# A fused attention and feed-forward kernel: first-batch stack copies moved in SP's queue, weight preparation moved to POOL, the batch loop written out

## The chip, the cores and the metric

One core of a Trainium2 chip. The metric is the time of one launch in microseconds (us), as the device reports it; lower is better. Engines: TensorE (PE in the profile, PEld its weight loads), VectorE (DVE), ScalarE (ACT), GpSimd (POOL), and SyncE (SP), which here only issues DMAs.

## What is computed

16 batches of 256 tokens with 512 features go through an attention block whose input is scaled and shifted by a condition vector, and then through a feed-forward block with ternary weights:

```
scale, shift = split(emb @ W_emb + b_emb)
xn = rms_norm(x) * g_norm * (1 + scale) + shift
q, k, v = heads(xn @ W_qkv)                  # 16 heads of 32
q, k = rms_norm(q) * g_q, rms_norm(k) * g_k
attn = softmax(q @ k.T * 32 ** -0.5)
o = attn @ v
y = o + o @ W_out
h = gelu(quant(layer_norm(y)) @ ternary(w_fc).T)
out = x + quant(layer_norm(h)) @ ternary(w_proj).T
ternary(w) = sign(round(w / mean(|w|))) * mean(|w|)
```

Everything is float32 at the boundary. Products are kept exact enough by splitting an operand into a float16 part "hi" and a float16 rest "lo".

## The kernel before

Each engine has its own instruction stream, written out by hand; semaphores order them. One iteration i works on several batches at once: the last products of batch i-2 (`late`), the feed-forward block of i-1 (`ffn`), the attention of i (`att`), Q, K and V of i+1 (`qkv`), and the rms norm of i+2 (`pre`). Iterations run from -2 to 17. `run` (line 434) calls them; iterations 3 to 13 are one body in a loop (`Fori`) on every engine, the others are written out.

An iteration has a first half (y = o + o @ W_out, norms, row maxima of the logits in four groups, eight units of the feed-forward block) and a head loop over h = 0 to 15: scores of head h on TensorE (line 831), exp and p_hi on ScalarE (1118, 1124), p_lo on VectorE (1448), products with v on TensorE (846 to 848). Scores of head h wait for the p_lo of two heads before, since they share a PSUM bank. Into the head loop the tables at lines 56 to 102 put other work by head number: pieces of Q, K and V (`FILLER`, and `SECOND_FILLER` for iteration 0), square sums, norms, transposes through the bank `T`, and in iteration 0 the preparation of the ternary weights: rounding (1037 on ScalarE, 1223 on VectorE), cutting (1232, 1234), signs (1048).

The first batch has no earlier batch to hide behind. Iteration -1 computes its Q, K and V while the weights are still coming in; iteration 0 takes the row maxima and then its scores. Scores are products of a stack `stk`: q and k parts of all heads, copied there by 16 DMAs from `qkT` (lines 570, 572), and one row with the negated maxima, `mrow` (written by VectorE at line 1420), copied by one DMA (`maxima_row`, 518). SP issues all DMAs in program order. Ahead of the stack copies of iteration -1 stand two for the rms norm of batch 1: the row `rx` to DRAM (558) and, when that has landed, its spread over all partitions, `rx_all` (560). VectorE multiplies the input of batch 1 by it (`scale_input`, 1372) in iteration 0, after `mrow` (unit 5 of the first half), then takes `xn_lo` (1277), with ScalarE's `xn_hi` (1056) between.

The output weight lies in `wo_raw`; VectorE adds the identity to it (1255), POOL writes `wo_hi` (610), VectorE `wo_lo` (1258). `magnitude` (1236) turns the summed absolute values of a weight into its scale in four one-element instructions; `proj_magnitude` (1263) does so for the second weight, and three more values.

```
sp.wait_ge(rx_r, nth(pre, 1, 1))
sp.dma_start(rx_row, rx[:, :]).then_inc(ld_row, 16)
sp.wait_ge(ld_row, nth(pre, 16, 0))
sp.dma_start(rx_all[:, :], rx_row...partition_broadcast(P)).then_inc(ld_all, 16)
...
sp.wait_ge(unturned, turn(i, ("piece", 3)) + 1)
```

## Time and profile before

| | |
|---|---|
| median of 3 runs | 1115.36 us (1114.02 to 1115.59) |
| the profiled execution | 1115.01 us, span 1113.2 us |
| TensorE busy | 1060.0 us (95%) |
| VectorE busy | 865.1 us (78%) |
| ScalarE busy | 806.7 us (72%) |
| POOL busy | 548.8 us (49%) |
| granted TensorE clock, mean | 0.981 |
| TensorE's share of the chain that ended last | 87% |

All times of rows are from the span's start. A matmul's end is modelled, so TensorE's busy time counts overlapping matmuls once but is no measure of its peak. The profile's page cuts the span into 40 slices of 27.8 us; stages shorter than that have to be asked for by their own window.

### The profile page before, as it was taken

The numbers are of one execution on the slowest core, as the hardware profiler recorded it, in microseconds if no ns is written. First come the engines' busy times: TensorE is split into PE (matmuls) and PEld (weight loads), VectorE is DVE, ScalarE is ACT, GpSimd is POOL, SyncE is SP. The second block draws the span as 40 slices with busy tenths as digits, with TensorE's granted clock in tenths as the row PEclk, the third lists the DMA queues.
The fourth block names the chain that finished last, engine by engine and source line by source line (L and its number), as shares of the span: only waits on it lengthen the run. The fifth ranks groups of instructions, "written<-read, shape, count | busy, mean of one in ns | idle before, by whom it ended". The sixth has DMA issues, their size and how long they took to land.

```text
span 1113.2 us, 26273 instructions
## 1 busy us (share of the span) xinstructions
PE 1060.0 (95%) x9457; PEld 668.5 (60%) x9457; DVE 865.1 (78%) x1617; ACT 806.7 (72%) x1371; POOL 548.8 (49%) x360
## 2 busy tenths in 40 slices
PE   8548899999999999999999999999999999999898
PEld 2225566656666565666666576666656666666565
DVE  4778768788887878788787878878787887877656
ACT  4758685868768586877868687786858688594954
POOL 1542291845629083653809265481917447181613
PEclk9769899999999999999999999999999999999999
DMA  9821313131121323112131312113131211212100
GB/s 355 293 58 20 81 26 77 58 74 58 31 78 42 75 62 75 57 34 66 42 94 43 75 57 44 55 42 94 43 75 57 54 64 27 54 40 58 58 21 19
DMA packets 79837, 76.18 MB, mean 68 GB/s; under 512 B 9008, under 2 KB 60336, under 8 KB 79280
## 3 DMA queue, kind: packets, MB, share of 16 engines
q1 hardware_dynamic: 79792, 75.58, 23.7%
q8 instruction: 29, 0.48, 0.2%
q14 instruction: 16, 0.13, 0.0%
HBM read 41.85 MB, written 8.40 MB: 45 GB/s over the span
## 4 chain that ended last, share of the span: by engine, by line
PE 87%; DVE 4%; ACT 4%; DMA 2%; issue 2%; POOL 1%; SPq 0%; ACTq 0%; DVEq 0%
PE F L939 10%; PE F L940 10%; PE F L772 9%; PE F L774 9%; PE QA L705 3%; PE QA L706 3%; PE QA L707 3%; PE QB L705 3%; PE QB L706 3%; PE QB L707 3%; PE T L985 3%; PE SB L831 2%; PE SA L831 2%; PE PV L848 2%; PE PV L847 2%; PE PV L846 2%
## 5 line engine op out<-in xcount | busy, mean ns | idle before, releaser
L939 PE MATMUL F<-yT_hi,fc_t 128*128 128x256 f16 x1024 | 228.6, 274 | 0.0
L940 PE MATMUL F<-yT_lo,fc_t 128*128 128x256 f16 x1024 | 228.2, 274 | 0.0
L655 POOL TENSOR_TENSOR rqk<-ssq,half 128x16 f32<-128x16 f32 x64 | 193.6, 3032 | 44.3 <-DVE ssq L1467 44.3
L772 PE MATMUL F<-proj_t,hs 128*128 128x512 f16 x512 | 194.1, 379 | 0.0
L774 PE MATMUL F<-proj_t,hs 128*128 128x512 f16 x512 | 193.7, 378 | 0.0
L624 POOL TENSOR_TENSOR acc<-acc,hg 128x512 f32<-128x512 f32 x96 | 152.5, 1588 | 11.4 <-ACT hg L1102 2.8
L1431 DVE SCALAR_TENSOR_TENSOR hs<-hg,g_inv,hs 128x512 f16<-128x512 f32 x128 | 110.9, 866 | 57.8 <-ACT hs L1107 57.6
L1102 ACT ACTIVATE hg<-F,g_fc 128x512 f32<-128x512 f32 x128 | 87.3, 682 | 52.6 <-PE F L940 51.0
L624 POOL TENSOR_TENSOR acc<-hg 128x512 f32<-128x512 f32 x16 | 20.3, 1270 | 212.7 <-DVE hs L1431 177.1
L631 POOL TENSOR_TENSOR acc<-acc,hq 128x512 f32<-128x512 f32 x90 | 114.2, 1269 | 13.3 <-ACT hq L1171 5.0
L618 POOL TENSOR_TENSOR rs<-var,half 128x1 f32<-128x1 f32 x32 | 17.6, 551 | 208.3 <-DVE var L1301 208.3
L1448 DVE TENSOR_TENSOR p_lo<-SA,p_hi 128x512 f16<-128x512 f32 x124 | 85.4, 688 | 42.0 <-ACT p_hi L1124 41.8
L939 PEld LDWEIGHTS F<-yT_hi,fc_t 128*128 128x128 f16 x1024 | 100.8, 98 | 18.6 <-issue 6.5
L846 PEld LDWEIGHTS PV<-v_hi,p_hi 128*128 128x128 f16 x1024 | 88.2, 96 | 33.9 <-issue 4.9
L940 PEld LDWEIGHTS F<-yT_lo,fc_t 128*128 128x128 f16 x1024 | 100.7, 98 | 11.9
L846 PE MATMUL PV<-v_hi,p_hi 128*128 128x33 f16 x1024 | 104.5, 178 | 2.8 <-DVE o_sb L1323 2.7
L1448 DVE TENSOR_TENSOR p_lo<-SB,p_hi 128x512 f16<-128x512 f32 x124 | 85.0, 685 | 26.3 <-ACT p_hi L1124 26.3
L848 PE MATMUL PV<-v_hi,p_lo 128*128 128x33 f16 x1024 | 103.6, 177 | 0.0
L847 PE MATMUL PV<-v_lo,p_hi 128*128 128x32 f16 x1024 | 103.4, 177 | 0.0
L847 PEld LDWEIGHTS PV<-v_lo,p_hi 128*128 128x128 f16 x1024 | 83.6, 96 | 24.9 <-issue 0.3
L1107 ACT ACTIVATE hs<-hg,g_inv 128x512 f16<-128x512 f32 x128 | 92.4, 722 | 5.1
L1118 ACT ACTIVATE SA<-SA 128x512 f32<-128x512 f32 x124 | 73.1, 590 | 21.8 <-PE SA L831 21.0
(226 smaller groups left out, 2724.0 us busy)
## 6 DMA issues: line engine op xcount, KB each, us to landing
stk<-qkT SPq DMA_DIRECT2D x128, 128.0 KB, 2.4
xtok<-in_x SPq DMA_DIRECT2D x17, 512.0 KB, 3.4
xT_sb<-in_xT SPq DMA_DIRECT2D x16, 512.0 KB, 3.3
stk<-qkT SPq DMA_DIRECT2D x128, 64.0 KB, 2.1
xres<-in_x SPq DMA_DIRECT2D x15, 512.0 KB, 3.2
out<-xres SPq DMA_DIRECT2D x15, 512.0 KB, 2.9
stk<-in_w_emb SPq DMA_DIRECT2D x4, 512.0 KB, 6.6
fc_t<-in_w_qkv SPq DMA_DIRECT2D x2, 1024.0 KB, 10.7
```

The lines of the kernel that those rows point to most:

```text
L624: pool.tensor_tensor(acc[:, 0, :], hg[:, 0, :] if n == 1 else acc[:, 0, :], hg[:, n, :], ALU.add).then_inc(sumh_r, 1)
L631: pool.tensor_tensor(acc[:, 1, :], hq[:, 0, :] if n == 1 else acc[:, 1, :], hq[:, n, :], ALU.add).then_inc(sumq_r, 1)
L655: pool.tensor_tensor(rqk[:, n % 2, :], ssq[:, n % 2, :], half[:, :], ALU.pow).then_inc(rqk_r, 1)
L772: pe.matmul(FB[t][:, :], hs[:, 0, k // 2, col:col + P], proj_t[:, k, :], start=(k == 0), stop=False)
L774: mm = pe.matmul(FB[t][:, :], hs[:, 1, k // 2, col:col + P], proj_t[:, k, :], start=False, stop=(k == FT - 1))
L846: pe.matmul(dst, ph, v_hi[:, k, h, :], start=(k == 0), stop=False)
L847: pe.matmul(dst[:, 0:DH], ph, v_lo[:, k, h, :], start=False, stop=False)
L848: mm = pe.matmul(dst, p_lo[:, h % (BEHIND + 1), k, t * P:(t + 1) * P], v_hi[:, k, h, :], start=False, stop=(k == TT - 1))
L939: pe.matmul(dst, w, yT_hi[:, k, :], start=(k == 0), stop=False)
L940: mm = pe.matmul(dst, w, yT_lo[:, k, :], start=False, stop=(k == KT - 1))
L1431: dve.scalar_tensor_tensor(hs[:, 1, n, :], hg[:, n, :], g_inv[:, 0:1], hs[:, 0, n, :], ALU.mult, ALU.subtract).then_inc(hlo_r, 1)
L1448: dve.tensor_tensor(p_lo[:, h % (BEHIND + 1), :, :], score_bank(att, h)[:, :].rearrange("p (k n) -> p k n", k=TT), p_hi[:, h % (BEHIND + 1 ...
```

## The change

SP, iteration -1: the spread `rx_all` is issued after the 16 stack copies instead of ahead of them. POOL: the four additions to the output weight go from VectorE to POOL, ahead of `wo_hi`, and POOL rounds block 0 of the first feed-forward weight, which ScalarE did. VectorE, iteration 0: both weights' scales are computed ahead of `scale_input`; `xn_lo` (and ScalarE's `xn_hi`) come after the first scores. TensorE, iteration 0: no Q, K or V piece at heads 0 and 1; the pieces follow from head 2 on, and squares, norms and turns one or two heads later. Start: `wq_lo` of the second and third part is cut or moved, `cur_s` of batch 0 is computed ahead of the scaled input, `g_k` later with a load of its own, the condition and its weight are laid out with four rows to a partition. The batch loop is written out on all engines.

```diff
-SECOND_FILLER = {0: QKV[0][0:2], 1: QKV[0][2:4], 2: QKV[1][0:2], 3: QKV[1][2:4]}
-SECOND_SQUARE_AT, SECOND_NORM_AT = {2: 0, 4: 1, 7: 2, 10: 3}, {4: 0, 6: 1, 9: 2, 12: 3}
-SECOND_TURN_AT = {5: ("piece", 0), 6: ("heads", 0), 8: ("piece", 1), 10: ("heads", 1), 11: ("piece", 2),
-                  13: ("piece", 3), 15: ("heads", 2)}
+SECOND_FILLER = {2: QKV[0][0:2], 3: QKV[0][2:4], 4: QKV[1][0:2], 5: QKV[1][2:4], 6: QKV[2][0:2], 7: QKV[2][2:4],
+                 9: QKV[3][0:2], 10: QKV[3][2:4], 12: V[0][0:2], 14: V[0][2:3], 15: V[0][3:4] + V[1][0:1]}
+SECOND_SQUARE_AT, SECOND_NORM_AT = {3: 0, 5: 1, 8: 2, 11: 3}, {5: 0, 7: 1, 10: 2, 13: 3}
+SECOND_TURN_AT = {6: ("heads", 0), 7: ("piece", 0), 9: ("piece", 1), 10: ("heads", 1), 12: ("piece", 2),
+                  14: ("piece", 3), 15: ("heads", 2)}
...
-WO_ADD_AT, WO_LOW_AT = 0, 3
+WO_LOW_AT, G_K_AT = 2, 3
...
-ACT_ROUND_AT = {0: 0, 1: 1}
+ACT_ROUND_AT = {1: 1}
...
-WQ_LOW_UNIT, WQ_LOW_AT = {0: 0, 2: 1}, 2
+WQ_LOW_UNIT, WQ_LOW_AT = {0: (0, 0, KT), 2: (1, 0, KT // 2)}, {1: (1, KT // 2, KT), 2: (2, 0, KT)}
...
             last_weights()
-            iteration(1)
-            iteration(2)
-            with engine.Fori(3, B - 2) as i:
+            for i in range(1, B + 2):
                 iteration(i)
...
                     sp.dma_start(rx_row, rx[:, :]).then_inc(ld_row, 16)
-                    sp.wait_ge(ld_row, nth(pre, 16, 0))
-                    sp.dma_start(rx_all[:, :], rx_row.rearrange("p t -> (p t)").partition_broadcast(P)).then_inc(ld_all, 16)
+                    if not held(pre):
+                        spread_rms(pre)
...
+                if held(pre):
+                    spread_rms(pre)
...
                 pool.memset(stk[MROW:STACK_ROWS, :, 1, :], 1.0).then_inc(s_ones, 1)
+                pool.wait_ge(s_ones, 1)
+                pool.wait_ge(ld_wo, 16)
+                for k in range(KT):
+                    blk = wo_raw[:, k * D + k * P:k * D + (k + 1) * P]
+                    pool.tensor_tensor(blk, blk, ident[:, :], ALU.add).then_inc(wo_i, 1)
                 pool.wait_ge(wo_i, KT)
                 pool.tensor_scalar(wo_hi[:, :, :].rearrange("p k n -> p (k n)"), wo_raw, WO_SCALE, None, ALU.mult
                                    ).then_inc(wo_h, 1)
+                pool.wait_ge(s_thr, 2)
+                pool.wait_ge(s_abs, 4)
+                pool.tensor_scalar(ffn_raw[0][0], ffn_raw[0][0], inv[:, 0:1], MAGIC, ALU.mult, ALU.add
+                                   ).then_inc(fc_round, 1)
...
                     if n == MAX_TURN_UNIT and held(qkv):
+                        magnitude(0)
+                        proj_magnitude()
                         for k in range(KT):
                             scale_input(qkv, k)
                         input_gain(pre)
-                        for k in range(KT):
-                            input_lo(qkv, k)
-                        magnitude(0)
...
-                    if isinstance(i, int) and i == 0 and h == WO_ADD_AT:
-                        out_weights("add")
...
+                    if held(qkv) and h == 0:
+                        for k in range(KT):
+                            input_lo(qkv, k)
```

SP's queue around the first batch's stack copies, before (`rx_row`, `rx_all`: the rms row and its spread; `stk`: the stack; `mrow`: the maxima):

```order
L558 DMA rx_row<-rx 128x2
L560 DMA rx_all<-rx_row 128x256
L570 DMA stk<-qkT 32x4x256 x2
L572 DMA stk<-qkT 32x8x256 x2
L570 DMA stk<-qkT 32x4x256 x2
L572 DMA stk<-qkT 32x8x256 x2
L570 DMA stk<-qkT 32x4x256 x2
L572 DMA stk<-qkT 32x8x256 x2
L570 DMA stk<-qkT 32x4x256 x2
L572 DMA stk<-qkT 32x8x256 x2
L518 DMA stk<-mrow 1x16x256
```

and with the change:

```order
L560 DMA rx_row<-rx 128x2
L572 DMA stk<-qkT 32x4x256 x2
L574 DMA stk<-qkT 32x8x256 x2
L572 DMA stk<-qkT 32x4x256 x2
L574 DMA stk<-qkT 32x8x256 x2
L572 DMA stk<-qkT 32x4x256 x2
L574 DMA stk<-qkT 32x8x256 x2
L572 DMA stk<-qkT 32x4x256 x2
L574 DMA stk<-qkT 32x8x256 x2
L516 DMA rx_all<-rx_row 128x256
L520 DMA stk<-mrow 1x16x256
```

The 16 copies have passed the spread; the row of maxima comes right after the spread, as the last of them all.

VectorE in iteration 0, from the scaled input of batch 1 on, before (`xT_sb<-xT_sb,cur_a,rx_all` is `scale_input`, `gam`, `den` and `inv` the weight's scale, `fc_t<-fc_t,ident` the additions to the output weight, `hs<-hs,inv` and `hg<-hg,inv` roundings):

```order
L1372 SCALAR_TENSOR_TENSOR xT_sb<-xT_sb,cur_a,rx_all 128x256 x4
L1362 TENSOR_SCALAR cur_a<-mod_a 128x4
L1277 SCALAR_TENSOR_TENSOR xn_lo<-xT_sb,cur_s,xn_hi 128x256 x4
L1238 TENSOR_REDUCE gam<-F 128x1
L1240 TENSOR_SCALAR gam<-gam 128x1
L1244 TENSOR_SCALAR den<-gam 128x1
L1246 RECIPROCAL inv<-den 128x1
L1448 TENSOR_TENSOR p_lo<-SA,p_hi 128x512
L1255 TENSOR_TENSOR fc_t<-fc_t,ident 128x128 x4
L1223 TENSOR_SCALAR hs<-hs,inv 128x2048
L1448 TENSOR_TENSOR p_lo<-SB,p_hi 128x512
L1223 TENSOR_SCALAR hg<-hg,inv 128x2048
```

and with the change, from the second weight's scale on (the first one's four instructions stand ahead of it):

```order
L1250 TENSOR_REDUCE gam<-F 128x1
L1252 TENSOR_SCALAR gam<-gam 128x1
L1256 TENSOR_SCALAR den<-gam 128x1
L1258 RECIPROCAL inv<-den 128x1
L1269 TENSOR_SCALAR g_fc<-gam 128x1
L1270 RECIPROCAL g_inv<-gam 128x1
L1271 SCALAR_TENSOR_TENSOR g_both<-gam 128x1
L1382 SCALAR_TENSOR_TENSOR xT_sb<-xT_sb,cur_a,rx_all 128x256 x4
L1372 TENSOR_SCALAR cur_a<-mod_a 128x4
L1454 TENSOR_TENSOR p_lo<-SA,p_hi 128x512
L1281 SCALAR_TENSOR_TENSOR xn_lo<-xT_sb,cur_s,xn_hi 128x256 x4
L1235 TENSOR_SCALAR hs<-hs,inv 128x2048
```

Both scales are now ahead of the scaled input, and xn_lo is behind the first p_lo; the additions are gone.

POOL around its first-weights block, with the change (before, the second and the fourth of these were not there; `proj_t<-proj_t,inv` is the rounding of fc block 0):

```order
L608 MEMSET stk 1x16x256
L613 TENSOR_TENSOR fc_t<-fc_t,ident 128x128 x4
L615 TENSOR_SCALAR wo_hi<-fc_t 128x2048
L619 TENSOR_SCALAR proj_t<-proj_t,inv 128x2048
L660 TENSOR_TENSOR rx<-msx,half 128x2
```

POOL's four additions stand between the memset and wo_hi, and its rounding behind wo_hi.

## Rows read from the trace of the kernel before

**Rows 1.** By stage: length; busy us (count) of PE, PEld, DVE, ACT, POOL; clock; DMA
```profile
52.40:62.80 10.40, 0.15 (x1) 0.06 (x2) 4.05 (x13) 1.70 (x4) 0.00 (x0) 0.50 0.68 157
62.80:111.80 49.00, 36.44 (x337) 20.89 (x338) 42.82 (x68) 38.81 (x52) 20.33 (x6) 0.85 0.09 23
313.00:377.00 64.00, 63.87 (x587) 40.99 (x585) 51.74 (x97) 48.22 (x84) 34.08 (x22) 1.00 0.22 60
```
**Rows 2.** The chain of waits, 30 to 64 us: start, duration, what
```profile
38.84 11.02 DMA rx_row<-rx
```
**Rows 3.** SP's timeline, 30 to 64 us: start, us, queue, line, DMA, how many
```profile
38.84 2.15 SPq L558 DMA_DIRECT2D rx_row<-rx  x1
49.88 0.34 SPq L560 DMA_DIRECT2D rx_all<-rx_row  x1
50.33 1.38 SPq L570 DMA_DIRECT2D stk<-qkT  x2
...
60.87 0.61 SPq L518 DMA_DIRECT2D stk<-mrow  x1
```
**Rows 4.** DMA issues, 50 to 62 us: KB each, us from issue to landing
```profile
rx_all<-rx_row SPq DMA_DIRECT2D x1, 128.0 KB, 3.4
stk<-mrow SPq DMA_DIRECT2D x1, 8.0 KB, 1.9
```
**Rows 5.** TensorE's timeline at the first scores; in brackets the idle time before
```profile
62.83 0.58 PE L831 MATMUL SA<-stk 97*128 97x256 f16 x2 [10.28 <-issue]
```
**Rows 6.** VectorE's timeline, first batch
```profile
41.54 0.96 DVE L1379 TENSOR_SCALAR cur_s<-mod_s 128x4 f32<-128x4 f32 x1
...
51.94 0.41 DVE L1420 TENSOR_SCALAR mrow<-T 16x256 f16<-16x256 f32 x1 [0.69 <-PE T L948]
53.34 1.67 DVE L1372 SCALAR_TENSOR_TENSOR xT_sb<-xT_sb,cur_a,rx_all 128x256 f32<-128x256 f32 x4 [0.98 <-DMA rx_all<-rx_row]
...
57.51 0.15 DVE L1240 TENSOR_SCALAR gam<-gam 128x1 f32<-128x1 f32 x1
57.70 0.15 DVE L1244 TENSOR_SCALAR den<-gam 128x1 f32<-128x1 f32 x1
...
64.76 0.69 DVE L1448 TENSOR_TENSOR p_lo<-SA,p_hi 128x512 f16<-128x512 f32 x1 [6.71 <-ACT p_hi L1124]
65.37 0.89 DVE L1255 TENSOR_TENSOR fc_t<-fc_t,ident 128x128 f32<-128x128 f32 x4
66.18 1.28 DVE L1223 TENSOR_SCALAR hs<-hs,inv 128x2048 f32<-128x2048 f32 x1
...
68.40 5.37 DVE L1223 TENSOR_SCALAR hg<-hg,inv 128x2048 f32<-128x2048 f32 x1
```
**Rows 7.** POOL's timeline, first batch
```profile
38.96 3.51 POOL L608 MEMSET stk<- 1x4096 f16 x1
...
66.34 6.34 POOL L610 TENSOR_SCALAR wo_hi<-fc_t 128x2048 f16<-128x2048 f32 x1 [23.88 <-DVE fc_t L1255]
```
**Rows 8.** ScalarE's timeline: a rounding
```profile
64.56 2.08 ACT L1037 ACTIVATE proj_t<-proj_t,magic,inv 128x2048 f32<-128x2048 f32 x1
```
**Rows 9.** ScalarE's timeline at the start
```profile
18.94 1.71 ACT L1056 ACTIVATE xn_hi<-xT_sb,cur_s 128x256 f16<-128x256 f32 x4 [0.97 <-DVE cur_s L1379]
```
**Rows 10.** TensorE's timeline: the same transposes in iterations 1, 3, 13, 14, 15
```profile
118.51 0.66 PE L788 MATMUL T<-ident,xn 128*128 128x128 f32 x4 [0.95 <-ACT xn L1078]
...
249.03 0.60 PE L788 MATMUL T<-ident,xn 128*128 128x128 f32 x4
...
891.62 0.60 PE L788 MATMUL T<-ident,xn 128*128 128x128 f32 x4
...
955.64 0.60 PE L788 MATMUL T<-ident,xn 128*128 128x128 f32 x4
...
1019.65 0.60 PE L788 MATMUL T<-ident,xn 128*128 128x128 f32 x4
```
**Rows 11.** DMA queues, 892 to 1020 us: packets, MB, share
```profile
q8 instruction: 5, 0.08, 0.3%
```

More of the change, by code:

```diff
@@ L138, in filler @@
 def filler(i, h):
-    if isinstance(i, int) and i == 0 and h < len(SECOND_FILLER):
-        return SECOND_FILLER[h]
+    if isinstance(i, int) and i == 0:
+        return SECOND_FILLER.get(h, [])
     if isinstance(i, int) and i < 0:
@@ L361, in adaln_ffn_kernel @@
         wq_l = sem("wq_l")
+        fc_round = sem("fc_round")
         wo_i = sem("wo_i")
@@ L432, in adaln_ffn_kernel, with run @@
         out_t = out.rearrange("b (t p) f -> b p t f", p=P)
-        def run(engine, iteration, qkv_weights, first_weights, last_weights):
+        def run(iteration, qkv_weights, first_weights, last_weights):
             iteration(-2)
@@ L578, in _ @@
                              w_qkv[:, w * D:(w + 1) * D].rearrange("(k p) n -> p k n", p=P)).then_inc(ld_wq[w], 16)
+            sp.dma_start(gqk_sb[:, :], g_qk).then_inc(ld_gqk, 16)
             iteration(-1)
-            iteration(0)
-            iteration(1)
-            iteration(2)
-            with sp.Fori(3, B - 2) as i:
-                iteration(i)
-            for i in range(B - 2, B + 2):
+            for i in range(B + 2):
                 iteration(i)
@@ L659, in iteration @@
                         pool.tensor_tensor(rs2[:, :], var2[:, :], half[:, 0:TT], ALU.pow).then_inc(rs2_r, 1)
-            run(pool, iteration, nothing, first_weights, nothing)
+            run(iteration, nothing, first_weights, nothing)
         @block.tensor
@@ L1013, in iteration @@
                     heads_turn(GROUPS - 1)
-            run(pe, iteration, nothing, nothing, nothing)
+            run(iteration, nothing, nothing, nothing)
         @block.scalar
@@ L1091, in iteration @@
                     input_squares(pre)
-                if held(qkv):
-                    input_hi(qkv)
                 if ffn is not None:
@@ L1149, in iteration @@
                         act.wait_ge(turned, turn(i, ("piece", n)) + 1)
+                        if n == 1 and first(qkv):
+                            act.wait_ge(s_gk, 1)
                         if n == 0 and live(qkv - 1):
@@ L1186, in _ @@
             act.preload_act_table(ACT.Exp)
-            act.wait_ge(s_gk, 1)
-            run(act, iteration, lambda: qkv_weights((0,)), nothing, lambda: act.wait_ge(s_gam, 7))
+            run(iteration, lambda: qkv_weights((0,)), nothing, lambda: act.wait_ge(s_gam, 7))
         @block.vector
         def _(dve):
-            dve.wait_ge(ld_const, 48)
+            dve.wait_ge(ld_const, 32)
             dve.wait_ge(c_pool, C_POOL)
-            dve.tensor_tensor(g_k[:, :], gqk_sb[:, 0:1], gqk_sb[:, 1:2], ALU.mult).then_inc(s_gk, 1)
             dve.tensor_scalar(bemb_sb[:, 0:KT], bemb_sb[:, 0:KT], 1.0, None, ALU.add).then_inc(s_bemb, 1)
@@ L1212, in _, with wq_low @@
             dve.wait_ge(s_mod, 2 * KT)
-            def wq_low(w):
+            def wq_low(w, k0, k1):
                 dve.wait_ge(wq_h, w + 1)
-                dve.scalar_tensor_tensor(wq_lo[:, :, w * D:(w + 1) * D], wq_raw[w].rearrange("p (k n) -> p k n", k=KT),
-                                         WQ_SCALE, wq_hi[:, :, w * D:(w + 1) * D], ALU.mult, ALU.subtract
-                                         ).then_inc(wq_l, 1)
+                rows, cols = slice(k0, k1), slice(w * D, (w + 1) * D)
+                dve.scalar_tensor_tensor(wq_lo[:, rows, cols],
+                                         wq_raw[w].rearrange("p (k n) -> p k n", k=KT)[:, rows, :], WQ_SCALE,
+                                         wq_hi[:, rows, cols], ALU.mult, ALU.subtract).then_inc(wq_l, 1)
             def dve_round(w, k):
@@ L1357, in add_squares, with input_shift @@
                                   ).then_inc(sumq_r, 1)
+            def input_shift(b):
+                if live(b - 1):
+                    dve.wait_ge(xlo_r, nth(b - 1, KT, KT))
+                dve.tensor_scalar(cur_s[:, :], mod_s[:, :, bass.ds(b, 1)].rearrange("p k o -> p (k o)"),
+                                  XQ_SCALE, None, ALU.mult).then_inc(cur_s_r, 1)
             def input_gain(b):
@@ L1375, in iteration @@
                 late, ffn, att, qkv, pre = stages(i)
-                if qkv is not None:
-                    if live(qkv - 1):
-                        dve.wait_ge(xlo_r, nth(qkv - 1, KT, KT))
-                    dve.tensor_scalar(cur_s[:, :], mod_s[:, :, bass.ds(qkv, 1)].rearrange("p k o -> p (k o)"),
-                                      XQ_SCALE, None, ALU.mult).then_inc(cur_s_r, 1)
+                if qkv is not None and not first(qkv):
+                    input_shift(qkv)
                 if pre is not None and not held(qkv):
@@ L1425, in iteration @@
                         input_gain(pre)
-                        for k in range(KT):
-                            input_lo(qkv, k)
-                        magnitude(0)
                     if ffn is not None:
@@ L1539, in iteration @@
                     value_lo(qkv, 1)
-            run(dve, iteration, nothing, nothing, last_weights)
+            run(iteration, nothing, nothing, last_weights)
 def kernel(x, cond_2048, L0_cond_W_emb, L0_cond_b_emb, L0_cond_g_norm, L0_cond_W_qkv, L0_cond_g_q, L0_cond_g_k,
```

63 lines of the change are left out of this document (33 added, 30 removed).

## The prediction

> **What bounds the kernel now.** I first read the busy time by stage [rows 1]. In the steady part TensorE is busy for 63.87 of 64.00 us: what the change does to the other engines there can't show, unless it takes something off TensorE's own instruction stream. The two stages before look different. Between 52.4 and 62.8 us no engine has much to do (VectorE 4.05 of 10.40 us, TensorE 0.15), and in the head loop of the first batch, 62.8 to 111.8, TensorE has 36.44 us of work in 49.00, VectorE 42.82, ScalarE 38.81. So the time lies in a hold before the first scores, then in a head loop that VectorE comes nearest to filling.
>
> The chain of waits names the hold [rows 2]: 11.02 us on the transfer of the rms row. SP's own timeline says who stands behind it [rows 3]. The row leaves at 38.84, behind the bulk loads, and SP stands at the spread (line 560) until 49.88. Only then come the 16 stack copies, from 50.33 on, and the row of maxima at 60.87, 10.54 us later, or 0.66 us for a copy. That row takes 1.9 us to land [rows 4], and the scores start at 62.83 after 10.28 us in which TensorE did nothing [rows 5]. Its operands had been there for long: the maxima were written by 52.35 (51.94 + 0.41) [rows 6].
>
> **Part 1: stack copies ahead of the spread.** The 16 copies need the last piece's low half, done when VectorE goes on at 41.54 [rows 6]; with the half microsecond of part 4 that is 41.1. The free queue takes a copy in 0.66 us, so the earliest end of the issues is 41.1 + 10.5 = 51.6. But the bulk loads hold the queue: the rms row, 1 KB, took 2.15 us to issue at 38.84, against 0.34 us for the spread on the free queue [rows 3], and landed only at 49.86. At the other end nothing is accepted before 49.8, and all is as before (60.3). I take a rate in between while the bulk lasts, about 1.1 us a copy, nearer to the fast end because the bulk drains all the while: 8 copies by 49.9, the other 8 at 0.66 us, done at 55.1. Then the spread (0.34), and the row of maxima at 55.5, on chip at 57.4. Scores at 57.5 in place of 62.8. The order of SP shows that only the copies pass the spread; the row of maxima stays behind it. That costs 0.4 us, since the rms row has landed by then.
> The price is on the spread: it is issued at 55.1, not 49.88, and lands 3.4 us later [rows 4], at 58.5 in place of 53.3. What needs it is the second batch's input: four scalings on VectorE of 1.67 us [rows 6], and these stand ahead of the first p_lo. So the first p_lo starts at 58.5 + 1.7 = 60.2 at the earliest.
>
> **Part 2: weights on POOL.** Removed from VectorE's head loop: four additions to the output weight, 0.89 us; the second weight's scale (seven one-element instructions, 0.19 us from start to start for a dependent one [rows 6], about 1.0 us); and a wait. The rounding of hg took 5.37 us, where the same instruction on hs took 1.28 [rows 6]: it lasted until POOL's wo_hi, 66.34 to 72.68 [rows 7], was over. That is 4.09 us. In the new order wo_hi needs only the output weight and the memset (over at 42.47), so it runs at about 43.5 to 50, under row maxima that VectorE reads from PSUM. Added to the loop: xn_lo, which used to lie in the hold, four instructions of the scalings' kind and size, 1.67 us [rows 6]. VectorE from its first p_lo to the stage's end: 111.8 - 64.76 = 47.0 us before, now 47.0 - 4.1 - 0.9 - 1.0 + 1.7 = 42.7. ScalarE loses one rounding of 2.08 us [rows 8] and gains xn_hi, of nearly the same length: no change, 38.8 us in a stage of 43 or more.
> New on POOL is the rounding of fc block 0. The nearest row is wo_hi, the same number of elements, 6.34 us [rows 7]. It may start as soon as the first scale is there: 51.85 (maxima row, half a microsecond early) + 4 x 0.19 = 52.6, so 52.7 to 59.0. **Here the change adds a wait.** Right behind that scale VectorE has the second one, with one-element tensor_scalars from SBUF to SBUF. Whether POOL holds these back no row shows. From below: nothing, as they take 0.15 us on a free chip [rows 6]. From above: cur_s at 41.54, 128x4 and normally some 0.16 us, took 0.96 and ended at 42.50, just after POOL's memset at 42.47 [rows 6, 7], and hg was held to the end of wo_hi. cur_s is the nearer row in size and kind, so I take the hold: VectorE goes on at 59.0, has 1.0 us of scale left, scales the input from 60.0 to 61.7 and starts the first p_lo at 61.7, not 60.2.
> The Trainium skill (Advanced Engine Details and Errata, GPSIMD Details) says that POOL shares a read and a write interface with VectorE and conflicts with its two-port mode; the two held rows agree, and by that rule my hold stands if one element per partition engages that mode. Against the move speaks the skill's GPSIMD Engine Reference (Key points): VectorE is about twice as fast at elementwise work. By that factor the POOL rounding would last about 2.6 us and the hold would vanish under the spread; the rows say 6.34 against 1.28 us, a factor of five, and the measurement decides.
>
> Sum for the stage: 61.7 + 42.7 = 104.4 in place of 111.8, so **-7.4 us**. It supposes that VectorE idles as much as before. The scores' start itself isn't what ends last any more: 57.5 + 1.9 (exp and p_hi, as from 62.83 to 64.76) is 59.4, under the 61.7.
>
> **Part 3: the moved QKV pieces.** Heads 0 and 1 have none now, since the spread is late; the pieces go over heads 2 to 10. Same matmuls, 36.4 us of TensorE in a stage of about 43: nothing, as long as TensorE keeps a margin. The granted clock was 0.50 in the hold and 0.85 in the loop [rows 1], that is, part of it at 1.2 GHz. The hold gets shorter, but early heads have less to do; I give it 1 us either way.
>
> **Part 4: the start.** cur_s before the four scalings: ScalarE waited 0.97 us for it [rows 9], most of which was the scalings themselves; 0.1 us is left, and ScalarE starts 0.4 us earlier. Of the second wq_lo only half now stands ahead of VectorE's first square sum. POOL's four powers then run without a gap to 38.1, so what the first one gains goes through, until a wait for the third: 0.5 us, which is in the times above. From below 0, from above 1.0. The fewer, longer packets of the condition are inside this.
>
> **Part 5: the loop written out.** Iterations 3 to 13 were one body with ten jumps back. Ten periods from 249.03 to 891.62 are 64.26 us each, the next two, 64.02 and 64.01, have no jump between them [rows 10]. So ten times 0.25: **-2.5 us**, on TensorE's path. These two fetch instructions, 5 packets of 16 KB [rows 11], and aren't slower for it. Bounds 1 to 3 us.
> The skill's Runtime: NRT & Kernel Launch (Instruction fetch mechanics) says a taken branch outside the fetched pages stalls; 0.25 us a jump is small for that, and the sum stays as it is.
>
> Sum: -7.4 - 2.5 = -9.9 us against the profiled execution's 1115.01, so **1105.1 us**. Its span is 1113.2, with 1.8 us around it that I keep. The median of the runs shown is 1115.36, 0.35 higher, well inside the range.
>
> **Rivals.**
> *No hold by POOL.* The first p_lo starts at 60.2, the stage ends 1.5 us earlier: 1103.6. If the copies also issue at the full rate, scores at 54, spread landed at 55, first p_lo at 56.7: -12.4 - 2.5, so 1100.1, the low end. For it: one-element instructions may not use what a long one uses. Against: cur_s.
> *The stage doesn't shrink.* ScalarE had 38.81 of 49 us of work and hands p_hi over head by head; TensorE now has its pieces late. If their coupling keeps the 47.0 us, the gain is only that of the start: 61.7 + 47.0 = 108.7, -3.1 - 2.5, so 1109.4. For it: both engines are over three quarters full. Against: a good part of the waits stood right behind the held rounding.
> *Slower: fetching instructions.* From 118.51 to 249.03, the first two written-out iterations took 130.5 us [rows 10], 2.5 over twice 64.0. If that were fetching, in a way that ten more iterations now share, it would cost up to 10 x 2.5 = 25 us on top of the forecast, 1130. It decides from 1.0 us an iteration, where it eats the 9.9 us. Against: iteration 14 is written out too and takes 64.01 [rows 10], and the granted clock in the first loop shows another cause for the early loss [rows 1].
>
> **Chances.** Forecast 0.48, no hold 0.24, stage doesn't shrink 0.24, fetching 0.04. What a measurement of this kernel can tell from no change is about 0.2%, 2.2 us. The first three cases lie 5.7 us and more below; of the third, a slow start of the copies could bring it near, which is worth 0.03. Faster 0.93, same 0.04, slower 0.03. The range runs from the low end of the second case to just above the third: 1100.0 to 1110.5.
>
> **What would show it.** Copies on SP from about 41, the maxima row at about 55; scores at 57.5; in VectorE's timeline a one-element gam or den instruction of about 6 us under POOL's rounding (right), or of 0.15 us (the second case); no 5.37 us rounding; the first y matmul near 104 in place of 111.8; all middle periods at 64.0. I am wrong if the scores start after 61, if the time from the first p_lo to the y matmul is still 47 us, or if periods grow.

## The result, and the profile after

| | before | after |
|---|---|---|
| median | 1115.36 us (1113.85 to 1115.79, 5 runs) | 1108.6 us (1107.74 to 1111.55, 5 runs) |
| profiled execution, span | 1115.01, 1113.2 us | 1109.38, 1107.5 us |

The ratio is 0.9948, 95% interval 0.9937 to 0.996: 6.8 us gained by the medians, 5.7 us between the two spans, where 9.9 were forecast. The time lies inside the range, but nearer to the rival *the stage doesn't shrink* (1109.4 us) than to the forecast (1105.1). The loss against the forecast is in the first batch's head loop. Three names recur: `ssq` is the square sum of a Q or K piece on VectorE, `rqk` the power that POOL takes of it, and `qkn` the piece normalised with it on VectorE; `QA` and `QB` are the two banks in which the pieces lie. An instruction is held when it lasts until another engine's instruction is over; the hold before the first scores is the stretch in which TensorE waits for the stack. These are the points at which I compare the traces, from their timelines:

| us from the span's start | before | after | change |
|---|---|---|---|
| mrow | 51.94 | 53.33 | +1.39 |
| first scores | 62.83 | 57.68 | -5.15 |
| first p_lo | 64.76 | 59.54 | -5.22 |
| third QKV piece of batch 1 starts | 80.66 | 77.66 | -3.00 |
| first y matmul, the stage's end | 111.77 | 109.14 | -2.63 |
| transposes of iteration 3 | 249.03 | 246.00 | -3.03 |
| transposes of iteration 13 | 891.62 | 885.57 | -6.05 |

So 5.2 us are won before the first p_lo, 2.6 of them are given back before the stage ends, and 3.0 come from the loop. The stages of the changed kernel, columns as in [rows 1]:

```profile
54.25:57.70 3.45, 0.02 (x1) 0.05 (x2) 2.29 (x9) 0.00 (x0) 1.98 (x1) 0.50 0.56 135
57.70:109.20 51.50, 38.40 (x337) 20.70 (x338) 40.22 (x66) 38.73 (x55) 15.16 (x5) 0.81 0.06 16
313.00:377.00 64.00, 63.93 (x588) 41.16 (x586) 51.45 (x99) 48.21 (x85) 34.09 (x22) 1.00 0.23 61
```

VectorE has 2.6 us less to do in the head loop than before, and yet the loop is 2.5 us longer (51.50 against 49.00). TensorE is busy for 38.40 us with the same 337 matmuls that took 36.44 before, at a granted clock of 0.81 in place of 0.85. The prediction counts the stage from the first p_lo to the first y matmul; here is that stretch before, then with the change:

```profile
64.76:111.77 47.01, 34.48 (x330) 19.84 (x329) 42.79 (x68) 37.53 (x50) 20.33 (x6) 0.86 0.07 14
```
```profile
59.54:109.14 49.60, 37.35 (x333) 20.26 (x334) 38.58 (x61) 37.53 (x53) 15.16 (x5) 0.82 0.06 17
```

In it VectorE's work fell by 4.2 us, and its idle time rose from 4.2 to 11.0.

SP's timeline shows the copies ahead of the spread, where [rows 3] had them behind it:

```profile
40.23 0.55 SPq L560 DMA_DIRECT2D rx_row<-rx  x1
43.04 1.37 SPq L572 DMA_DIRECT2D stk<-qkT  x2
...
53.00 1.25 SPq L574 DMA_DIRECT2D stk<-qkT  x2
54.30 0.60 SPq L516 DMA_DIRECT2D rx_all<-rx_row  x1
54.95 0.57 SPq L520 DMA_DIRECT2D stk<-mrow  x1
```

TensorE's timeline, the rows that answer to [rows 5] and [rows 10]:

```profile
57.68 0.58 PE L842 MATMUL SA<-stk 97*128 97x256 f16 x2 [3.74 <-issue]
...
61.87 0.61 PE L714 MATMUL QA<-wq_hi,xn_hi 128*128 128x512 f16 x1 [0.91 <-DVE xn_lo L1281]
...
77.66 0.61 PE L714 MATMUL QA<-wq_hi,xn_hi 128*128 128x512 f16 x1 [5.05 <-DVE qkn L1480]
...
109.14 0.38 PE L714 MATMUL SA<-wo_hi,oT_hi 128*128 128x512 f16 x1
...
246.00 0.60 PE L799 MATMUL T<-ident,xn 128*128 128x128 f32 x4
...
885.57 0.60 PE L799 MATMUL T<-ident,xn 128*128 128x128 f32 x4
```

The longest idle time of TensorE in the stage is the 5.05 us at 77.66: the third piece needs the bank that qkn reads. VectorE's timeline, which answers to [rows 6], shows who is late:

```profile
53.33 0.41 DVE L1427 TENSOR_SCALAR mrow<-T 16x256 f16<-16x256 f32 x1 [0.69 <-PE T L959]
...
54.62 0.15 DVE L1252 TENSOR_SCALAR gam<-gam 128x1 f32<-128x1 f32 x1
54.81 0.15 DVE L1256 TENSOR_SCALAR den<-gam 128x1 f32<-128x1 f32 x1
...
55.33 1.13 DVE L1271 SCALAR_TENSOR_TENSOR g_both<-gam 128x1 f32<-128x1 f32 x1
57.45 1.67 DVE L1382 SCALAR_TENSOR_TENSOR xT_sb<-xT_sb,cur_a,rx_all 128x256 f32<-128x256 f32 x4 [0.98 <-DMA rx_all<-rx_row]
...
59.54 0.69 DVE L1454 TENSOR_TENSOR p_lo<-SA,p_hi 128x512 f16<-128x512 f32 x1 [0.22 <-ACT p_hi L1133]
...
63.53 1.28 DVE L1235 TENSOR_SCALAR hg<-hg,inv 128x2048 f32<-128x2048 f32 x1
...
68.82 0.69 DVE L1476 TENSOR_REDUCE ssq<-sq 128x16 f32<-128x528 f32 x1
71.48 0.69 DVE L1454 TENSOR_TENSOR p_lo<-SA,p_hi 128x512 f16<-128x512 f32 x1 [1.97 <-ACT p_hi L1133]
72.09 1.22 DVE L1244 TENSOR_SCALAR fc_t<-proj_t 128x2048 f16<-128x2048 f32 x1
...
76.92 0.68 DVE L1480 TENSOR_TENSOR qkn<-QA,rqk 128x512 f32<-128x512 f32 x1
```

Three things are to be seen. The one-element gam and den run in 0.15 us although POOL's rounding has begun at 54.48; g_both, a scalar_tensor_tensor (two inputs), takes 1.13 in place of 0.14 and ends with it at 56.46. Without POOL's rounding (e7 below) it takes 0.14. So VectorE was held after all, for 1.0 us, but not on the path: it then waited for the spread, which landed at 57.45. The rounding of hg takes 1.28 us, the 5.37 are gone. And between the first piece's square sum at 68.82 and its qkn at 76.92 lie 8.10 us, where before (75.30 and 79.92) there were 4.62. POOL's timeline, for [rows 7]:

```profile
25.77 13.77 POOL L664 TENSOR_TENSOR rqk<-ssq,half 128x16 f32<-128x16 f32 x4 [10.01 <-DVE ssq L1476]
...
45.72 5.37 POOL L615 TENSOR_SCALAR wo_hi<-fc_t 128x2048 f16<-128x2048 f32 x1
54.48 1.98 POOL L619 TENSOR_SCALAR proj_t<-proj_t,inv 128x2048 f32<-128x2048 f32 x1 [3.39 <-DVE inv L1258]
...
69.59 3.76 POOL L664 TENSOR_TENSOR rqk<-ssq,half 128x16 f32<-128x16 f32 x1 [0.70 <-DVE ssq L1476]
```

The power that qkn waits for is over at 73.35. From there on qkn waits 3.57 us for nothing but its own engine: between the square sum and qkn VectorE's order has a p_lo, two cuts, a rounding, the heads' output, the next p_lo and the next square sum.

The start, where mrow lost 1.4 us, in VectorE's timeline:

```profile
24.99 0.70 DVE L1476 TENSOR_REDUCE ssq<-sq 128x16 f32<-128x528 f32 x1 [0.80 <-ACT sq L1145]
25.61 1.21 DVE L1228 SCALAR_TENSOR_TENSOR wq_lo<-fc_t,wq_hi 128x1024 f16<-128x1024 f32 x1
```

in TensorE's:

```profile
26.88 0.60 PE L740 MATMUL QB<-wq_lo,xn_hi 128*128 128x512 f16 x2 [1.22 <-DVE wq_lo L1228]
```

and in ScalarE's:

```profile
27.52 0.60 ACT L1145 ACTIVATE sq<-QB 128x512 f32<-128x512 f32 x1 [1.20 <-PE QB L740]
```

The first square sum did not come earlier with only half a wq_lo ahead of it (24.99, before 24.93): it waits 0.80 us for ScalarE's square. ScalarE's own wait for VectorE shrank from 0.97 to 0.69 us, but its xn_hi began at 19.17 in place of 18.94. The second half, now behind it, ends at 26.82, and the second piece's last products wait for that half. Its square starts at 27.52 in place of 26.13.

### The profile page after: what moved, and what is told of

It is laid out like the page before. It is cut to its first block, busy times and chain, and to the rows that moved or that the text cites. A ratio compares the mean times of both kernels' runs of the same rounds, so it can differ in the third digit from the quotient of the medians.

```text
span 1107.5 us, 24385 instructions
## 1 busy us (share of the span) xinstructions
PE 1060.1 (96%) x9457; PEld 668.5 (60%) x9457; DVE 854.9 (77%) x1614; ACT 804.6 (73%) x1370; POOL 553.8 (50%) x365
## 4 chain that ended last, share of the span: by engine, by line
PE 90%; DVE 4%; ACT 3%; issue 1%; POOL 1%; DMA 1%; SPq 0%; ACTq 0%; DVEq 0%
PE F L950 10%; PE F L951 10%; PE F L783 10%; PE F L785 10%; PE QA L714 4%; PE QA L715 4%; PE QA L716 4%; PE QB L714 3%; PE QB L715 3%; PE QB L716 3%; PE T L996 3%; PE SB L842 2%; PE SA L842 2%; PE PV L859 2%; PE PV L858 2%; PE PV L857 2%
## 5 line engine op out<-in xcount | busy, mean ns | idle before, releaser
L633 POOL TENSOR_TENSOR acc<-acc,hg 128x512 f32<-128x512 f32 x96 | 150.0, 1562 | 15.7 <-ACT hg L1111 2.8
L1437 DVE SCALAR_TENSOR_TENSOR hs<-hg,g_inv,hs 128x512 f16<-128x512 f32 x128 | 104.8, 819 | 64.8 <-ACT hs L1116 64.7
```

Source lines behind the costliest of these rows:

```text
L633: pool.tensor_tensor(acc[:, 0, :], hg[:, 0, :] if n == 1 else acc[:, 0, :], hg[:, n, :], ALU.add).then_inc(sumh_r, 1)
L1437: dve.scalar_tensor_tensor(hs[:, 1, n, :], hg[:, n, :], g_inv[:, 0:1], hs[:, 0, n, :], ALU.mult, ALU.subtract).then_inc(hlo_r, 1)
```

## The experiments

All were timed beside runs of the kernel before on the same chip; ratios are to it. The medians of that kernel lie between 1114.92 and 1115.52 us, so medians of different experiments can be compared to about 0.6 us. The theory at this point: (a) the loop is worth 3 us by itself; (b) the stage's first part ends with qkn, and what is gained ahead of it is lost in VectorE's own order; (c) the start's loss is the cut wq_lo. The main rival to (b) is that the three engines, each with some 40 us of work in 50, hold each other up everywhere.

**The loop alone**, on the kernel before:

```diff
-            iteration(1)
-            iteration(2)
-            with engine.Fori(3, B - 2) as i:
+            for i in range(1, B + 2):
                 iteration(i)
-            iteration(B - 2)
...
```

> The kernel before with only the batch loop written out on all engines. My theory (a jump back costs 0.25 us on TensorE's path, ten of them, and a little in the two iterations at the edges): 1115.2 - 3.0 = 1112.2 us, and all middle periods at 63.95. Rival (the faster periods of the changed kernel come from its other parts, or the extra instruction fetches cost what the jumps did): 1115 us or more. Second theory to tell apart: the gain is the ten jumps alone, -2.5, if the first period (66.36 before) stays.

Measured: 1111.81 us against 1115.14, ratio 0.9967 (0.9955 to 0.998). TensorE's timeline, iterations 3 and 13:

```profile
250.18 0.60 PE L777 MATMUL T<-ident,xn 128*128 128x128 f32 x4
...
889.63 0.60 PE L777 MATMUL T<-ident,xn 128*128 128x128 f32 x4
```

Ten periods of 63.95 us, against 64.26 in [rows 10]: 3.1 us in this trace, 3.0 in that of the changed kernel. The ten periods give 3.1 of the 3.3 us by the medians. The first two iterations have no part in it (130.95 us from the same transposes of iteration 1 to those of 3, before 130.52), and the added instruction fetches (75 and 39 packets on the two instruction queues, before 29 and 16) cost nothing that shows. How the 0.31 us a period divide between the jump and the loop's bookkeeping isn't shown.

**The copies alone**: the kernel before, with `spread_rms` behind the stack copies as in the change.

> The kernel before with only the spread of the rms row issued behind the 16 stack copies. Theory: scores at about 56.3 in place of 62.8, but the input's scaling, xn_hi and the exp that stands behind xn_hi on ScalarE put the first p_lo at about 61 in place of 64.8; with the 47.0 us that the stage had, -3.7 us, so 1111.5. Rival (what the stage gains at its start is lost at the wait for the first normalised piece, whose square sum hangs on other work): 1113.5 or more.

Measured: 1112.84 us against 1115.14, ratio 0.9981 (0.9971 to 0.999), -2.3 us by the medians, between the two expectations. Its profiled execution was one of the two slowest of ten (1115.07) and is no measure of the gain (scores at 59.73, but first p_lo only at 64.25, before 64.76). It does show a mechanism. SP's timeline:

```profile
41.47 1.38 SPq L574 DMA_DIRECT2D stk<-qkT  x2
...
49.12 3.19 SPq L574 DMA_DIRECT2D stk<-qkT  x2
```

Two copies took 3.19 us to issue here, and all sixteen 14.8, from 41.47 to 56.2. In the changed kernel they start 1.6 us later and take 11.2. When they end goes by the bulk loads ahead of them: here the last of these landed at 52.8 (issued at 36.84, 16.0 us), in the changed kernel at 50.8 (36.28, 14.5 us), and the copies ended 3.4 us after it in both. In all nine traces in which the copies stand behind the bulk, this distance is 3.1 to 3.5 us, with starts from 40.9 to 43.0.

**The cut wq_lo in one piece again**, on the changed kernel:

```diff
-WQ_LOW_UNIT, WQ_LOW_AT = {0: (0, 0, KT), 2: (1, 0, KT // 2)}, {1: (1, KT // 2, KT), 2: (2, 0, KT)}
-WQ_LOW_DONE = (1, 3, 4)
+WQ_LOW_UNIT, WQ_LOW_AT = {0: (0, 0, KT), 2: (1, 0, KT)}, {2: (2, 0, KT)}
+WQ_LOW_DONE = (1, 2, 3)
...
```

> The changed kernel with the second part of wq_lo in one piece again, ahead of VectorE's first square sum. Theory: the second piece's products wait for its lower half, which the change put behind the first square sum; undone, the square of the second piece starts at 26.2 in place of 27.5, POOL's four powers run on without a gap, and mrow and the stack copies come 1.3 us earlier: 1108.6 - 1.3 = 1107.3 us. Rival (the start is late because its loads landed 0.5 us later): no gain, 1108.6, or up to 0.4 us slower because the first square sum moves back.

Measured: 1108.24 us, ratio 0.9942 (0.9929 to 0.9956): no difference from the change's 0.9948 that can be told. The first half of the theory holds in its trace: the second square sum at 26.65 in place of 28.15, POOL's powers 12.46 us without a gap, mrow at 51.83 in place of 53.33, copies from 41.54. But they end at 54.0 all the same (54.25 before this edit), and the scores start at 57.41 in place of 57.68. The bulk loads absorbed 1.2 of the 1.5 us. The trace of e7 below, with wq_lo still cut, says the same: its copies start at 41.54 too and end at 54.34. So the sign of the start was wrong, and what it cost was small. In this execution the stretch from the first p_lo to the y matmul took 47.02 us at a granted clock of 0.87, where the change's trace has 49.60 at 0.82. The medians don't follow, so this is a difference between executions, and the 49.60 us of one trace are to be read with it.

**qkn one head earlier**, VectorE's order alone, on the changed kernel:

```diff
-... SECOND_NORM_AT = ..., {5: 0, 7: 1, 10: 2, 13: 3}
+... SECOND_NORM_AT = ..., {4: 0, 7: 1, 10: 2, 13: 3}
-FC_CUT_AT = {4: 0, 6: 1}
+FC_CUT_AT = {3: 0, 6: 1}
```

> The changed kernel, VectorE alone reordered: in iteration 0 the first normalised piece at head 4 instead of head 5, and the first cut of the ternary weight at head 3, where VectorE idles 1.97 us. Theory (the stage's length is set by when the third QKV piece can start, which waits for qkn of the first; from there to the stage's end it is 31.1 us before and 31.5 us after): qkn at 73.4 in place of 76.9, the third piece at 74.0 in place of 77.7, and 1108.6 - 3.6 = 1105.0 us. Rival (VectorE, ScalarE and TensorE hold each other up everywhere, each near 40 us of work in 50): the wait moves on to another place and the time stays at 1108.6, within 0.5 us.

Measured: 1105.44 us against 1115.14, ratio 0.9909 (0.9895 to 0.9923), 3.2 us under the change's 1108.6. VectorE's timeline, then TensorE's:

```profile
73.34 0.69 DVE L1480 TENSOR_TENSOR qkn<-QA,rqk 128x512 f32<-128x512 f32 x1 [1.47 <-POOL rqk L664]
```
```profile
74.09 0.61 PE L714 MATMUL QA<-wq_hi,xn_hi 128*128 128x512 f16 x1 [1.76 <-DVE qkn L1480]
```

qkn now follows POOL's power at once, and the third piece starts 3.57 us earlier. From there to the y matmul (at 105.08) it is 30.99 us, much as in the change (31.48). It isn't the clock: from the first p_lo to the y matmul it takes 45.63 us at 0.81, where the change took 49.60 at 0.82. The order of one engine's queue was worth half of what the whole change had brought; the rival, that the wait would move on and the time stay within 0.5 us, is out.

**POOL's rounding back on ScalarE**, on the changed kernel:

```diff
-ACT_ROUND_AT = {1: 1}
+ACT_ROUND_AT = {0: 0, 1: 1}
...
-                pool.tensor_scalar(ffn_raw[0][0], ffn_raw[0][0], inv[:, 0:1], MAGIC, ALU.mult, ALU.add
-                                   ).then_inc(fc_round, 1)
...
```

> The changed kernel with block 0 of the first feed-forward weight rounded on ScalarE at head 0 again, and no rounding on POOL. Theory (between the first p_lo and the third QKV piece, ScalarE with 8.1 us of work in 9.7 stands in the chain: its exp for head 1 lets the scores of head 3 and the QKV products behind them go): up to 2.1 us later, 1108.6 + 1.5 = 1110 us. Rival (POOL's rounding bought nothing, because the stage waits elsewhere): 1108.6, within 0.5.

Measured: 1108.25 us, ratio 0.9937 (0.9923 to 0.9951): the rival is right. The 2.1 us on ScalarE delay the first square sum (68.82 to 70.91), but qkn only from 76.92 to 77.60. VectorE's timeline shows the two-input instruction free of its hold:

```profile
53.84 0.14 DVE L1267 SCALAR_TENSOR_TENSOR g_both<-gam 128x1 f32<-128x1 f32 x1
```

While qkn stands behind VectorE's queue, that move bought nothing. What it would be worth with qkn moved up wasn't tried.

**What the hold was worth**, on the kernel before. It takes the result of the two probes below, that POOL's pass is short with two operations:

```diff
-                pool.tensor_scalar(wo_hi[...], wo_raw, WO_SCALE, None, ALU.mult
+                pool.tensor_scalar(wo_hi[...], wo_raw, WO_SCALE, 0.0, ALU.mult, ALU.add
```

> The kernel before with one edit: POOL's wo_hi as a scaling and an addition of 0.0, two operations, so that by the probes its pass takes about 2.0 us in place of 5.4 and lets VectorE's rounding of hg behind it start 3.4 us earlier. It prices the hold by itself. Theory (the hold stood ahead of the first square sum, and so ahead of qkn, the third QKV piece and the stage's end): hg 1.8 us or less in place of 5.4, the first square sum near 71.8 in place of 75.3, 1115.1 - 3.4 = 1111.7 us. Rival (the hold was hidden behind ScalarE and TensorE, and its removal gives back less than 1 us): 1114.5.

Measured: 1112.78 us against 1115.52, ratio 0.9975 (0.9966 to 0.9985), -2.7 us where the theory had -3.4 and the rival under -1. POOL's timeline and VectorE's:

```profile
66.74 2.87 POOL L610 TENSOR_SCALAR wo_hi<-fc_t 128x2048 f16<-128x2048 f32 x1 [24.30 <-DVE fc_t L1255]
```
```profile
68.79 1.90 DVE L1223 TENSOR_SCALAR hg<-hg,inv 128x2048 f32<-128x2048 f32 x1
```

From the first p_lo to the third piece it is now 13.12 us, before 15.90: the hold stood in the chain, and 3.5 us less of it (5.37 to 1.90) took 2.8 us off that part.

**Idle matmuls in the hold**, on e4's kernel:

```diff
                             weight_sums(1)
+                            keep_busy(SB[0], 8)
```

> The kernel of e4 with 8 idle matmuls of 512 columns on TensorE between the weight sums and the first scores, where it stands idle for 3.9 us. Theory (the first QKV piece of batch 1 is at the lower clock, 0.43 us a matmul, because TensorE had so little to do from 43 us on; work in the hold brings the clock back before 67.4): square sum and qkn of the first piece up to 2 us earlier, 1105.4 - 1.5 = 1104 us. Rival (3.5 us of work come too late to move the clock, or what ends last there is VectorE and POOL): 1105.4, within 0.5.

Measured: 1104.57 us, ratio 0.9906 (0.9892 to 0.992), which can't be told from e4's 0.9909. In its profiled execution the stretch from the third piece to the stage's end has a granted clock of 0.94 and takes 29.33 us, where e4 has 0.85 and 30.99. The kernels of e6 and e10, without idle matmuls, also have 0.94 there, and take 29.97 and 29.79. So the clock is worth 1 to 2 us in this stretch, and it isn't shown that the idle matmuls bring it.

**The edits of e3 and e4 together:**

> The edits of e3 and e4 together on the changed kernel. If they add up: 1105.4 - 0.4 = 1105.0 us, scores 0.2 us earlier only, since the stack copies that start 1.3 us earlier wait for the last bulk loads to drain and end at 54.0 all the same. Rival: the 1.3 us come through once the stage no longer waits for qkn, 1104.1.

Measured: 1105.35 us, ratio 0.9915 (0.9901 to 0.9929): the first expectation, 1105.0; the rival's 1104.1 lies just outside the interval. Scores at 56.83, copies from 40.88 to 53.2, 12.4 us for what the free queue does in 10.5. The last bulk load landed at 50.0, 0.8 earlier than in the changed kernel's trace, so the scores' lead is not the edit's alone.

**One bulk load less ahead of the copies**, on e6's kernel: the tokens of batch 2 behind the row of maxima, their square sums (ScalarE) at head 2, the mean (VectorE) and its power (POOL) at head 4.

```diff
                     maxima_row(i, att)
+                    input_tokens(pre)
...
-                    input_tokens(pre + 1)
```

> The kernel of e6 with the load of batch 2's tokens (512 KB) behind the row of maxima instead of ahead of the stack copies; its square sums at head 2, its mean at head 4. Theory (the end of the stack copies is set by when the bulk loads ahead of them drain, not by when they start): 512 KB less is some 1.4 us of the full rate, the copies end at about 52.7 in place of 53.5, scores and first p_lo 1 us earlier, 1105.4 - 1.0 = 1104.4 us. Rival (the copies are limited by their own 0.65 us each): no gain, or slower by up to 1 us for the 1.6 us of squares that ScalarE now has in the head loop.

Measured: 1104.25 us, ratio 0.9911 (0.9894 to 0.9927). The copies end at 52.49 in place of 53.2, the scores start at 56.17 in place of 56.83: the direction that was expected, 0.7 us in place of 1.0, and in the time too small to tell from e6. The next experiment's trace doesn't bear the 0.7 out.

**That, with the idle matmuls of e5:**

> The kernel of e10 with the 8 idle matmuls of e5. If both work, 1104.4 - 0.9 = 1103.5 us; if the idle matmuls of e5 did nothing and its 0.9 us was scatter of the clock, the same as e10.

Measured: 1103.44 us against 1114.92, ratio 0.9895 (0.9879 to 0.9912). It is the fastest of all and beats both kernels: 11.5 us under the kernel before, 5.2 under the change. Against e4 the intervals overlap. Of the 5.2 us only the 3.2 of e4 are shown one by one. In its trace the copies end at 53.36 and the scores start at 57.10, no earlier than in e6: with one load less ahead, the last one landed at 49.9, against 50.0 in e6 and 49.1 in e10. The copies follow the bulk's end again, by 3.5 us; that the load moved away brings that end forward isn't shown.

**POOL by itself.** Two probes behind the last store of the changed kernel, whose whole times mean nothing. The first:

```diff
+            pool.wait_ge(st_out, nth(B - 1, 16, 32))
...
+            pool.tensor_scalar(dst, src, WO_SCALE, None, ALU.mult).then_inc(pr_big, 1)
...
+            pool.tensor_scalar(src, src, inv[:, 0:1], MAGIC, ALU.mult, ALU.add).then_inc(pr_big, 1)
...
+            pool.tensor_scalar(src, src, WO_SCALE, None, ALU.mult).then_inc(pr_big, 1)
...
+            for n in range(PROBES):
+                dve.wait_ge(pr_go, n + 1)
+                held_op(n).then_inc(pr_done, 1)
```

> The changed kernel with a probe behind its last store: POOL passes over 128x2048 (to f16; to f32 in place with two operations; to f32 with one) while VectorE is idle, then eleven more, each with one VectorE instruction started under it; only the durations are of interest. Theory A (the output's type sets POOL's time): 5 us or more to f16, about 2 us to f32, with VectorE idle. Theory B (POOL's 5.4 to 6.3 us are VectorE's load on a shared port): all three about 2 us while VectorE is idle. On the hold: one-element tensor_scalar 0.15 us (not held), reciprocal likewise, 128x4 tensor_scalar and one-element scalar_tensor_tensor held to the end of POOL's pass; of the 128x512 ones I expect tensor_scalar and tensor_tensor held and the reduction not.

With VectorE idle: 5.37 us to f16 with one operation, 1.97 to f32 in place with two, 5.36 to f32 in place with one. (An operation is one arithmetic step of the instruction: a scaling alone, or a scaling and an addition.) Both theories fall: neither the output's type nor VectorE's load makes the 5.4 us. None of the eleven VectorE instructions was held; each had begun before, or within 0.1 us of, POOL's pass. There it was POOL that waited: its two-operation pass took 2.25 us against a 128x512 tensor_scalar and 2.52 against the two-input forms of that size.

The second puts a reduction ahead of each instruction in question, and tries other forms on POOL:

```diff
                 dve.wait_ge(pr_go, n + 1)
+                dve.tensor_reduce(den[:, 1:2], b, AX, ALU.add).then_inc(pr_red, 1)
                 held_op(n).then_inc(pr_done, 1)
```

> A second probe behind the last store of the changed kernel, since in the first VectorE's instruction had always begun before POOL's pass. Here VectorE first runs a reduction of 0.69 us (which did not lengthen POOL's pass) and then the instruction in question, so that it comes some 0.7 us into the pass. If a pass that already runs holds some kinds and not others: 128x4 tensor_scalar and one-element scalar_tensor_tensor last until POOL's end (up to 4.7 us under a 5.36 us pass), one-element tensor_scalar and reciprocal 0.15 us; the long SBUF-to-SBUF ones are held too, the reduction is not. Rival (no hold of this kind exists, what held hg and cur_s was something else): all at 0.15 to 0.69 us. And POOL's own time: if the number of operations sets it, one operation with a pointer 5.4 us and two with constants 2 us; if the pointer does, the other way round; to f16 with two operations 2 us if the output's type is without weight.

POOL's timeline of the second probe, its three forms and one of the passes of the test:

```profile
1105.95 5.45 POOL L675 TENSOR_SCALAR hg<-hg,inv 128x2048 f32<-128x2048 f32 x1 [7.55 <-DMA out<-xtok]
1111.49 1.90 POOL L677 TENSOR_SCALAR hg<-hg 128x2048 f32<-128x2048 f32 x1
1113.48 1.97 POOL L679 TENSOR_SCALAR hs<-hg,inv 128x2048 f16<-128x2048 f32 x1
...
1121.30 5.36 POOL L685 TENSOR_SCALAR hs<-hg 128x2048 f16<-128x2048 f32 x1
```

One operation with a pointer takes 5.45 us, two with constants 1.90, two to f16 1.97. In the six passes of the two probes the time goes with the number of operations alone. VectorE's timeline, some 0.6 us into a 5.36 us pass:

```profile
1116.25 0.14 DVE L1575 TENSOR_SCALAR hq<-hq 128x1 f32<-128x1 f32 x1
...
1121.85 4.84 DVE L1577 TENSOR_SCALAR hq<-hq 128x4 f32<-128x4 f32 x1
...
1127.55 3.09 DVE L1579 SCALAR_TENSOR_TENSOR hq<-hq 128x1 f32<-128x1 f32 x1
...
1133.15 0.15 DVE L1581 RECIPROCAL hq<-gam 128x1 f32<-128x1 f32 x1
```

Held are the 128x4 tensor_scalar and the scalar_tensor_tensor; the one-element tensor_scalar, the reciprocal and the reduction (0.68 us) are not. Under a memset the 128x4 one took 2.83 us, to the memset's end, and the scalar_tensor_tensor 0.15. The Trainium skill (SBUF — State Buffer, Who interferes with whom) says that a VectorE instruction contends in a two-port mode, or with two SBUF inputs against a POOL instruction that reads SBUF, and that whoever issues first keeps the pair of ports for the whole instruction. The probes agree, with one difference: under POOL's 5.36 us pass the two-input instructions came free after 3.6 us, not at its end. Under the pass of 1.97 us the scalar_tensor_tensor was held to the end (1.32 us), as g_both was in the changed kernel.

## Why the prediction was right or wrong

**What bounds the kernel:** right. The hold on the rms row was the largest loss ahead of the loop, and the middle batches have nothing to give but the loop itself.

**Part 1, the copies:** right at the end, and in part by luck on the way. Copies done at 54.25 (forecast 55.1), scores at 57.68 (57.5), spread landed at 57.45 (58.5). They started 1.9 us later than forecast (43.04 against 41.1) and took 11.2 us, not 14.0. The picture of a queue that runs at a rate in between while the bulk lasts was too smooth: most pairs went out in the 1.3 us of the free queue, and single ones took up to 3.2. The end goes by the landing of the last bulk load: the copies end 3.1 to 3.5 us after it in nine traces, with starts that differ by 2.2 us.

**Part 2, the hold by POOL's rounding:** wrong. "cur_s is the nearer row in size and kind, so I take the hold": cur_s has four elements, gam and den one, and by the second probe that decides for a tensor_scalar. The one instruction that was held is the two-input g_both, for 1.0 us and hidden under the spread. The first p_lo started at 59.54, not 61.7, after 0.22 us of waiting for ScalarE's p_hi; the rival *no hold by POOL* named 60.2. The pass itself was mis-sized, 6.34 forecast and 1.98 measured, because the nearest row was of one operation and this pass has two. By the factor of two in the Trainium skill's GPSIMD Engine Reference (Key points) the estimate was 2.6 us; there the page was nearer than the row that I set against it. And of the 6.34 us, 5.37 were POOL's own, as the changed kernel's row shows; the rest would fit a wait of POOL for VectorE's rounding of hs, which had begun 0.16 us earlier, but no run tests that.

**Part 2, the stage:** wrong. "VectorE from its first p_lo to the stage's end: ... now 47.0 - 4.1 - 0.9 - 1.0 + 1.7 = 42.7." It was 49.6. The terms themselves came true: in this stretch VectorE has 38.58 us of work in place of 42.79, 4.2 less where 4.3 were forecast, and hg takes 1.28. The step that failed is "It supposes that VectorE idles as much as before": the idle time went from 4.2 to 11.0 us. A sum of one engine's work is a stage's length only if that engine ends last throughout. Here the first part ended with qkn: from the first p_lo to the third piece 15.90 us before, 18.12 after (16.97 in e3's trace of nearly the same kernel). The removal of most of the hold takes 2.8 us off the first part in e12, so the other changes added some 4 to 5, an estimate from these four traces. From the third piece to the end it is 31.11 us before and 31.48 after, and that these agree is chance: the granted clock was 0.94 before and 0.89 after, and the four later kernels with 0.94 there (e5, e6, e10, e11) take 29.3 to 30.0.

**Part 3, the moved pieces:** "nothing, as long as TensorE keeps a margin" is the step that failed most. TensorE had the same 337 matmuls, at a lower clock: they kept it busy for 38.40 us in place of 36.44, 2.0 more, where the prediction gave the clock 1 us either way. But the larger loss is in the order. The first piece moved two heads later and its norm one head, from head 4 to 5, behind cuts and a rounding. Moving the norm back gave 3.57 of those us in the trace and 3.2 in the time (e4). The rival *the stage doesn't shrink* had the outcome ("if their coupling keeps the 47.0 us"; 49.60 in the change's trace, 47.02 in e3's), but not the cause: 3.2 us of it were one place in one queue.

**Part 4, the start:** wrong in sign, -0.5 forecast, +1.4 at mrow. "What the first one gains goes through" supposed that the first square sum waited for VectorE; it waited for ScalarE's square. The words "until a wait for the third" looked for the new wait in the wrong place; it is the second piece's. By e3 only about 0.3 us of it reached the scores.

**Part 5, the loop:** right in mechanism, and a little larger: 3.0 to 3.1 us over the ten periods, 3.3 in the time (e1), in place of 2.5. I took the two unrolled iterations of [rows 10], 64.02 and 64.01, as the floor; it is 63.95. *Fetching instructions* is out.

Together: first p_lo 5.2 us earlier where 3.1 were forecast, stage 2.6 longer where 4.3 less were forecast, loop 3.0 for 2.5. That the time lies within the range is in part luck: a first p_lo 2.2 us earlier than forecast hid part of a stage that was 6.9 us longer than forecast. In the rivals' paragraph the third case lies 5.6 us below by its own terms (3.1 + 2.5), not 5.7; nothing hangs on it. What stays open is how much of the changed kernel's gain beside copies and loop (6.8 - 2.3 - 3.3 = 1.2 us by the medians) belongs to which small edit, and what made the clock lower in its head loop.

## What to carry to other kernels

When work is moved to a later place, follow its result to the last consumer and look at what stands ahead of each link on that link's own engine: here an unchanged instruction count hid 3.2 us in the order of one queue. Take an engine's busy sum for a stage's length only where that engine ends each part of it. And before work is pulled forward onto a queue, look at what the queue is still draining: 1.5 us of earlier start were worth 0.3 (e3). Two stretches in one trace each are only comparable with their clocks beside them.
